# An adaLN transformer block on one core: matmuls of the identity in TensorE's waits, and exponentials, score copies and attention work moved forward in the first steps

## What is computed

```python
mod = (silu(c) @ wmod).reshape(8, 6, 1, -1)      # sa, ca, ga, sb, cb, gb; ga, gb kept away from 0
h = layernorm(x) * (1 + ca) + sa
q, k, v = (h @ W.T + b for q, k, v), 16 heads of 16 channels
raw = q @ k.T                                    # 512 x 512 for each head
scores = where(mask, raw, 0) / 4                 # mask: j == i or j == i - 2**n
x = x + ga * (softmax(scores) @ v @ Wo.T + bo)
h = layernorm(x) * (1 + cb) + sb
x = x + gb * (mxquant(h) @ mxquant(weight).T + bias)   # blocks of 32, grid of fp6 e2m3
```

## Time and profile before

| | us |
|---|---|
| median of 3 runs (lowest, highest) | 286.82 (286.75, 286.82) |
| the profiled execution | 286.72 |
| its span, from the first to the last instruction | 285.0 |
| outside the span | 1.7 |
| PE, DVE, ACT, POOL busy | 255.6, 258.8, 212.5, 210.5 |

### The profile page before, as it was taken

How to read it: one execution, slowest core, us unless ns; L and a number is a source line. 1 busy time by engine, 2 the same in 40 slices (tenths; PEclk the granted TensorE clock), 3 DMA queues, 4 the chain that set the end, 5 groups by cost and what they waited for, 6 DMA issues and landing times.

```text
span 285.0 us, 4442 instructions
## 1 busy us (share of the span) xinstructions
PE 255.6 (90%) x1368; PEld 158.8 (56%) x1368; DVE 258.8 (91%) x326; ACT 212.5 (75%) x577; POOL 210.5 (74%) x152
## 2 busy tenths in 40 slices
PE   6999997697978795989999999999999988997885
PEld 1653554175526561666556646664567646794663
DVE  3699799969995999999999999999999999999970
ACT  2386987975697779879898989887776937575752
POOL 7101439895879999999999999999999699845100
PEclk9999999999999999999999999999999999999999
DMA  7743977694784239724993389347943965730005
GB/s 225 193 181 81 340 248 232 230 338 133 240 273 148 73 125 350 251 72 131 295 336 127 129 263 286 135 113 222 333 147 94 279 198 178 230 103 11 0 26 199
DMA packets 54399, 53.91 MB, mean 189 GB/s; under 512 B 4100, under 2 KB 52824, under 8 KB 54376
## 3 DMA queue, kind: packets, MB, share of 16 engines
q1 hardware_dynamic: 54376, 53.63, 60.1%
HBM read 44.90 MB, written 8.72 MB: 188 GB/s over the span
## 4 chain that ended last, share of the span: by engine, by line
DVE 39%; POOL 19%; PE 18%; issue 11%; ACT 11%; DVEq 0%; POOLq 0%; ACTq 0%
POOL pv_buf L677 14%; DVE prod L1721 9%; DVE pv_buf L1851 9%; DVE prod L1851 4%; DVE prod L1710 4%; PE ps L988 3%; PE ps L1067 3%; PE ps L826 2%; ACT dump L1197 2%; PE ps L853 2%; ACT dump L1238 1%; DVE ps L1825 1%; PE ps L837 1%; DVE ps L1827 1%; POOL rstd L658 1%
## 5 line engine op out<-in xcount | busy, mean ns | idle before, releaser
L677 POOL TENSOR_TENSOR pv_buf<-pv_buf 128x1024 f32<-128x1024 f32 (+2 forms) x60 | 132.5, 2209 | 15.0 <-DVE pv_buf L1851 9.8
L1721 DVE TENSOR_TENSOR prod<-ps,kT 128x1024 f32<-128x1024 f32 (+4 forms) x70 | 75.1, 1110 | 0.0
L1851 DVE TENSOR_TENSOR pv_buf<-v_shift,ps 128x1024 f32<-128x1024 f32 x49 | 59.1, 1212 | 0.0
L937 PE MATMUL ps<-prod,sel_sum 128*32 128x512 f32 x256 | 30.8, 598 | 8.5 <-DVE prod L1721 7.8
L853 PE MATMUL ps<-wT,h_cen 128*128 128x256 f32 x128 | 29.9, 379 | 0.0
L826 PE MATMUL ps<-hT,wT 128*128 128x512 f32 x64 | 29.7, 596 | 0.0
L837 PE MATMUL ps<-hT,wT 128*128 128x512 f32 x64 | 29.3, 599 | 0.0
L988 PE MATMUL ps<-wo_g,w_raw 128*128 128x256 f32 x112 | 27.9, 392 | 0.0
L853 PEld LDWEIGHTS ps<-wT,h_cen 128*128 128x128 f32 x128 | 23.9, 190 | 6.4 <-issue 3.8
L988 PEld LDWEIGHTS ps<-wo_g,w_raw 128*128 128x128 f32 x112 | 20.1, 189 | 5.4 <-issue 3.2
L937 PEld LDWEIGHTS ps<-prod,sel_sum 128*32 128x32 f32 x256 | 6.7, 109 | 28.0 <-issue 13.8
(11 more groups left out here) (212 smaller groups left out, 550.3 us busy)
## 6 DMA issues: line engine op xcount, KB each, us to landing
v_shift<-v_rows SPq DMA_DIRECT2D x56, 512.0 KB, 5.7
x_in<-in_L_attn_x SPq DMA_DIRECT2D x8, 512.0 KB, 4.4
v_rows<-v_base SPq DMA_DIRECT2D x8, 512.0 KB, 4.1
x_res<-in_L_attn_x SPq DMA_DIRECT2D x8, 512.0 KB, 6.5
out_x<-outb SPq DMA_DIRECT2D x5, 512.0 KB, 5.8
rows_mod<-mod_rows SPq DMA_DIRECT2D x7, 256.0 KB, 3.4
x<-in_L_wmod SPq DMA_DIRECT2D x1, 1024.0 KB, 7.9
row_ga<-mod_rows SPq DMA_DIRECT2D x8, 128.0 KB, 4.9
```

What stands on the lines that cost most here:

```text
L677: nc.gpsimd.tensor_tensor(dst, dst, ring(b, n)[:, t:NT, :], ALU.add).then_inc(s_add, 1)
L937: mm = nc.tensor.matmul(ps23[32 * g:32 * g + 32, 1, :], sel_sum[:, which, c, :], prod[:, n, c, :], start=(c == 0 and which == 0), stop=(c ...
L1721: nc.vector.tensor_tensor(prod[:, n, :, o:L], ps01[:, :, o:L], kT[:, b % 2, :, 0:L - o], ALU.mult).then_inc(s_prod, 1)
L1851: nc.vector.tensor_tensor(dst[:, t:NT, :].rearrange("p t (h e) -> p t h e", e=DH), v_n.rearrange("p t (h e) -> p t h e", e=DH), weights, A ...
```

## The change

1. *Filling, PE.* The seven narrow matmuls are replaced by seven f32 matmuls of the 128x128 identity with itself (`warm_up`), 3 + 1 + 3; the first three start as soon as the identity stands.
2. *Steps 0 to 2, PE.* Such matmuls are put where PE waits: six ahead of `h_transposes(2)` in step 0 (`warm_in_step`), 2 + 2 (in steps 1 and 2: 1 + 1) ahead of `head_sums(b + 1, 1)` (`warm_by_products`), and two between `v_means` and `scores_by_token(b + 1)`.
3. *Filling, quantising of the weight.* DVE keeps three instructions; the two products go to POOL, the rounding to ACT.
4. *ACT.* `centre_h(1)` goes behind `exps(0)`. `norm_before(3)` leaves the end of step 0 for the middle of step 1, `norm_before(4)` the end of step 1 for the middle of step 2. `squares_after` goes in steps 1 and 2 from the end to right behind `take_x1`.
5. *POOL.* In step 0 `rstd_before(3)` goes behind add 9, and `gate_projection` in steps 0 and 1 too.

```diff
+            def scale_ffn_weight(src, factor, after):
+                pool.wait_ge(s_wfq, after)
+                nc.gpsimd.tensor_tensor(w_raw[:, 4, :, :].rearrange("p c (g k) -> p (c g) k", k=BLOCK),
+                                        src.rearrange("p (g k) -> p g k", k=BLOCK), over(factor[:, :], BLOCK),
+                                        ALU.mult).then_inc(s_wfq, 1)
...
             rstd_before(0)
+            scale_ffn_weight(w_raw[:, 4, :, :].rearrange("p c k -> p (c k)"), wf_inv, WF_SCALED - 1)
+            scale_ffn_weight(wf_q[:, :], wf_scale, WF_CODES)
             rstd_before(1)
...
                 add(b, 4)
-                gate_projection(b)
+                if b > 1:
+                    gate_projection(b)
                 add(b, 5)
                 add(b, 6)
                 if has(b + 3) and has(b - 1):
                     rstd_both(b)
-                elif has(b + 3):
-                    rstd_before(b + 3)
...
                 add(b, 9)
+                if b == 0:
+                    rstd_before(3)
+                if b < 2:
+                    gate_projection(b)
...
+            def warm_up(ps, bank, n):
+                for i in range(n):
+                    nc.tensor.matmul(ps[:, bank, 0:P], ident[:, :], ident[:, :], start=True, stop=True)
+
+            pe.wait_ge(s_const, 2)
+            warm_up(ps67, 1, 3)
...
-            keep_busy(ps67, 1, 3)
+            warm_up(ps67, 1, 1)
...
-            keep_busy(ps67, 1, 4)
+            warm_up(ps67, 1, 3)
...
+            def warm_in_step(b, n):
+                pe.wait_ge(s_d, b + 1)
+                if b > 0:
+                    pe.wait_ge(s_x1, b)
+                warm_up(ps67, 1, n)
+
+            def warm_by_products(b, n):
+                for made in (6, 7):
+                    pe.wait_ge(s_prod, NO * (b + 1) + made)
+                    warm_in_step(b, n)
...
                 v_rows(b + 1, 0)
+                if b == 0:
+                    warm_in_step(0, 6)
...
+                if b < TAIL - 1:
+                    warm_by_products(b, 2 if b == 0 else 1)
                 head_sums(b + 1, 1)
                 head_sums(b + 1, 2)
                 v_means(b)
+                if b < TAIL - 1:
+                    warm_in_step(b, 2)
                 scores_by_token(b + 1)
...
+            def ffn_weight_codes():
+                act.wait_ge(s_wfq, WF_SCALED)
...
             evacuate_k(0, 0)
+            ffn_weight_codes()
             sums_before(1)
...
-            centre_h(1)
 
             for b in range(LAST - 1):
                 exps(b)
+                if b == 0:
+                    centre_h(1)
...
                 evacuate_v(b + 1, 1)
+                if 0 < b < TAIL - 1:
+                    norm_before(b + 2)
...
                     take_x1(b - 1)
+                    if b < TAIL - 1:
+                        squares_after(b - 1)
...
-                if has(b - 1):
+                if has(b - 1) and b >= TAIL - 1:
                     squares_after(b - 1)
...
-                if has(b + 3):
+                if b >= TAIL - 2 and has(b + 3):
                     norm_before(b + 3)
```

More of the change, by code:

```diff
@@ L203, in adaln_block @@
         s_xtiled = sem("first_x_norm_tiles_by_vector")
+        s_wfq = sem("ffn_weight_quantising_step")
         s_split = sem("gated_biases_split")
@@ L290, in adaln_block @@
         CONST_ALL = CONST_SUM + NO + 2
-        SETUP_SILU, SETUP_COLS, SETUP_WF, SETUP_MOD, SETUP_ROWS = 3, 5, 11, 12, 16
+        SETUP_SILU, SETUP_COLS, SETUP_MOD, SETUP_ROWS = 3, 5, 6, 10
+        WF_SCALED, WF_CODES, WF_DONE = 4, 5, 6
         PE_COND, PE_MOD, PE_WK, PE_COLS, PE_WQ, PE_WV, PE_ROWS, PE_WO, PE_WF = range(1, 10)
@@ L777, in weight_transposes @@
                 if i == 4:
-                    pe.wait_ge(s_cset, SETUP_WF)
+                    pe.wait_ge(s_wfq, WF_DONE)
                     pe.wait_ge(s_x1, 1)
@@ L1169, in evacuate_weight @@
                 nc.scalar.activation(wT[:, i, :, :], turned_weight(i), ACT.Copy).then_inc(s_wTe, 1)
+            def ffn_weight_codes():
+                act.wait_ge(s_wfq, WF_SCALED)
+                act.wait_ge(s_const, 3)
+                nc.scalar.activation(wf_q[:, :], w_raw[:, 4, :, :].rearrange("p c k -> p (c k)"), ACT.Identity,
+                                     bias=tie[:, 0:1], saturate=False).then_inc(s_wfq, 1)
             def norm(src, dst, rstd, shift, done, tiles=slice(0, NT)):
@@ L1519, in _ @@
                     seed_q(b + 2)
-                if has(b + 3):
+                if b >= TAIL - 2 and has(b + 3):
                     norm_before(b + 3)
-                elif has(b - 1):
+                elif b >= TAIL - 2 and has(b - 1):
                     norm_after(b - 1)
@@ L1670, in setup_rows @@
                 link, k = chain(s_cset, 0, 0)
-                k[0] = SETUP_WF
+                k[0] = SETUP_COLS
                 dve.wait_ge(s_pset, PE_ROWS)
@@ L1686, in setup_rows, with ffn_weight_scales @@
                 assert k[0] == SETUP_ROWS
-            def setup_ffn_weight():
-                link, k = chain(s_cset, 0, 0)
-                k[0] = SETUP_COLS
+            def ffn_weight_scales():
                 dve.wait_ge(s_w_in[4], 16)
-                dve.wait_ge(s_const, 3)
                 wf_b = w_raw[:, 4, :, :].rearrange("p c (g k) -> p (c g) k", k=BLOCK)
[L1695 to L1704, removed]
+                nc.vector.tensor_reduce(wf_amax[:, :], wf_b, AX_X, ALU.max,
+                                        apply_absolute_value=True).then_inc(s_wfq, 1)
+                dve.wait_ge(s_wfq, 1)
+                nc.vector.tensor_scalar(wf_scale[:, :], wf_amax[:, :], TO_E4M3 / FP6_MAX, TO_E4M3 * MX_EPS,
+                                        ALU.mult, ALU.max).then_inc(s_wfq, 1)
+                dve.wait_ge(s_wfq, 2)
+                nc.vector.reciprocal(wf_inv[:, :], wf_scale[:, :]).then_inc(s_wfq, 1)
             def first_qk_products(c):
@@ L1853, in pv_product @@
                                         ALU.mult).then_inc(s_pv, 1)
-            setup_ffn_weight()
+            ffn_weight_scales()
             first_qk_products(1)
```

## The result

| | median us (range, runs) | ratio to before (95%) |
|---|---|---|
| before | 286.78 (286.54 to 286.82, 4) | |
| changed | 293.17 (290.11 to 293.83, 4) | 1.0204 (1.0131 to 1.0276) |

The changed kernel is 2% slower; 284.0 was forecast. Its profiled execution took 290.11 (span 288.4), the shortest of the four; the others had spans of 291.2 to 292.1. Several kernels, that of before too, have single executions that take 2 to 3 us more at a mean clock under 1 (two took far more, 304.33 and 436.81), so a median of few runs carries a microsecond of doubt and more, and the profiles are read beside it.

The account below looks back on a forecast made before the run. DVE was taken to set the time up to add 6 of step 1, with DVE, PE and POOL all full later. 1.8 (filling) + 1.0 (POOL) = 2.8 us off 286.82 gave 284.0, range 283.0 to 285.6.

Parts of the forecast that it names:

- Quantising off DVE, warm-up (1.8): Filling: first product on DVE earlier by 1.8 us, bounds 0.75 and 2.45, through less DVE work and an earlier full clock.
- rival B: Filling: the clock rises no earlier, so the gain is 0.75 + 1.0 = 1.75 us and the time 285.1; chance 17%.
- Exponentials (1.15 and 2.05): DVE's waits for ACT's exponentials shrink to about 0.13: 1.15 us won in step 0, 2.05 in step 1.
- POOL (1.0): Adds of step 2 on POOL: 2.3 us earlier less 1.3 for the moved gate_projection(1), net 1.0.
- all full engines keep this distance: Behind step 2: nothing is changed there, so the 2.8 us won stay to the end.
- SP: SP's list: load_x(4) goes later, lands at 72.5 to 74.6, ACT may wait up to 2.3 us; it fits, barely.
- Fillers (cost 0, gain 0): Identity matmuls in PE's waits of steps 0 to 2: cost 0, at most 0.5 us in step 1, gain 0.
- Rival F: Slower: load_x(4) lands late and holds POOL's root and all later steps; 287.8 for a landing at 79; chance 4%.
- limit of 74.6: Landing of load_x(4) in us, behind which every microsecond holds POOL's root and all later steps.
- the issue at 68.5: SP's list: load_x(4), issued at 62.62 before, was to go at about 68.5 us.
- POOL's arrival at 85.2: Step 1: POOL comes for the variance its root needs at 82.85 + 2.36 = 85.2 us.

Follow-up runs that it names:

- the filling alone: The kernel before with only the seven identity matmuls in the filling and the quantising off DVE, all steps as before; 286.82 us, ratio 0.9986.
- the gate in place: The changed kernel with gate_projection of steps 0 and 1 put back between adds 4 and 5; 284.93 us, ratio 0.9930.
- the gate late and the transfer free: The changed kernel, gate_projection still behind add 9, with SP's list altered in two ways; 287.80 and 287.21 us.
- the two ways: Two versions of the changed kernel, each with another order of transfers around load_x in SP's list; 287.80 and 287.21 us.
- the gate's place alone: The kernel before with only gate_projection of steps 0 and 1 moved behind add 9; 293.36 us, ratio 1.0221.
- the first way: The changed kernel with load_row_ga of steps 1 and 2 sent behind load_x in SP's list; 287.80 us, ratio 0.9989.
- the second way: The changed kernel with load_row_ga left in its place and the three shift_v behind it sent after load_x; 287.21 us, ratio 1.0011.

## Why the prediction was wrong, step by step

- **Quantising off DVE, warm-up (1.8).** In the first profile it gave 16.55 - 14.97 = 1.58. But it stands on the clock: the x transposes took 1.09 in seven of the eleven profiles with identity matmuls there, and 1.63 to 1.97 in the other four, among them the second run of the changed kernel and the filling alone (rival B). In medians the filling alone gives nothing that can be told.
- **Exponentials (1.15 and 2.05).** Right in place and nearly in size: waits of 0.21 each, where 0.13 was assumed. That add 6 of step 1 comes at 81.08 for 81.05 is in part luck: the filling gave 1.58 for 1.8, and `softmax_max(1)` came 0.52 earlier beyond that, for 0.2.
- **POOL (1.0).** Not reached here. With the gate in place the adds of step 2 come 3.5 earlier, with the gate late and the transfer free 2.8 (97.03 and 97.02 in the two ways; 97.0 was forecast). So this term was right for a kernel whose transfer is not late. That "all full engines keep this distance" did not hold: in both ways `softmax_max(4)` is only 1.2 earlier than before (147.12 and 147.11 for 148.28), behind the low clock of step 3; with that wait filled it is 2.5 earlier.
- **SP: this step failed.** "Transfers into `x_in` land after 3.2 to 6.1 us ... at 72.5 to 74.6 ... ACT ... may wait up to 2.3 us ... It fits, barely." I took the range of landings from transfers that ran in other company, while I had myself written that three others stand ahead. The three were held until 65.3 and then released at once, with `load_x(4)` and `spill_v` right behind; 512 KB took 8.5 us, ACT waited 5.48. Sizes and rate were to be had before: five times 512 KB at some 370 GB/s are 7 us.
- **Fillers (cost 0, gain 0): failed too.** "The clock shows no fall to be prevented" is true of the profile before, even behind its wait of 2.77 us, but says nothing of a kernel whose waits lie elsewhere. In the changed kernels the clock does fall; the step fillers are worth about 1.5 us where the gate is in place, and filling step 3's wait kept 1.35 at `softmax_max(4)`. That a wait of PE brings the fall is shown for step 3 alone.
- **Rival F** had the mechanism, at 4%, and its slope holds. Its limit of 74.6 is reckoned without the 1.8 won in the filling, like the issue at 68.5 and POOL's arrival at 85.2; on the changed kernel's own axis the limit is 72.8. The landing, 67.25 + 8.5 = 75.75, was 2.95 behind it, and POOL's root waited 3.24. By F that makes 284.0 + 2.95 = 287. (Its 287.8 for a landing at 79 is a slip: 284.0 + 4.4 = 288.4.) What F lacked came on top: ACT's residual stands behind the sums that wait, so PE ran dry; the clock fell; and ACT's norm was late for POOL (1.98). Three microseconds behind the limit cost five at POOL.
- Shown: the gate's place alone makes the loss; moving transfers around `load_x(4)` alone removes it. Shown for one place, step 3, by one profile and four runs: filling PE's wait keeps the clock. Shown by one pair of profiles: that the low clock near 82 is 2.6 of the 9.20.
- Open: the microsecond in the tail (clock 0.96 from 250 to 270, 0.95 from 270 to 288, where before had 1.00), and most of the 2 us by which leaving the step fillers out helps when the transfer is late. The stretch behind `softmax_max(7)`, which the change doesn't touch, took 45.4 us of the span in the profiles of before and of the filling alone and 48.3 in that of the first way, with clock 0.50 from 265 to 270: a total of one execution says less than the time at `softmax_max(7)`.

Four versions beat both kernels: the gate in place (284.93; 284.93 with three matmuls more; 285.14 with narrow ones in the filling), and the gate late with shifts behind `load_x` and step 3's wait filled (284.74). A fifth, the gate in place without step fillers, does so only just (286.53). The simplest is the first, 0.7% under before.

## What to carry to other kernels

When an instruction moves, follow the semaphore that it raises into the DMA queue: a transfer held there releases all those behind it at once, and they land at the shared rate, so price the last of them by the bytes of the crowd, not by the range of landings seen so far. A full clock in the profile before says nothing of waits that PE didn't have before; where a change moves or lengthens them, price the work behind at half speed as well. Move cheap work out of an engine's slack only after asking who needs its result, since here 1.3 us of POOL's work, moved out of a wait, cost 6 us through the transfers behind it.

## What the runs showed of the hardware

- The same program at the same place doesn't always get the same clock. The changed kernel with the gate in place and the second way have equal waits of PE (0.48 and 0.97) ahead of 68.8, and before them one of 0.74 in the first and of 0.36 in the second; from 70 to 74 the first had 0.66, the second 1.00. Whether the longer of the two waits or chance decides, no run separates. In the filling the same identity matmuls were followed by x transposes of 1.09 us in seven profiles and of 1.63, 1.94, 1.97 and 1.97 in four.
- Behind PE's waits of 2.74 and 2.75 us in step 3, the clock was 0.57 and 0.58 over four microseconds, with PE busy for all four. That such a short wait in a full engine can go with half speed I had not expected. It need not: the 2.77 us of the kernel before were followed by clock 1.00.
- In the filling alone the level rose within L798, at 11.27, and from 8.12 on PE had run little but transposes: as in the prediction, this does not agree with the Trainium skill, "TensorE: Matmul & The Clock Gate", section "Part 4: PE-mode transpose", by which transposes don't count.
- The granted clock of the view can miss the lower level at the start: in the profile before it reads 1.00 from 4 to 12 us, while four transposes take 1.12 and 1.06 us there and 0.60 from 15.68 on the earlier trace rows. In the filling the level has to be read from durations.
